# Attention weights made transposed by a second score product, in place of six transposes

## The chip, the cores and the metric

The kernel runs on one core of a Trainium2 chip. The metric is the device time of the whole program in microseconds (us), measured outside the profiler; three executions of the kernel before gave 4838.08, 4842.09 and 4854.21, so the median is 4842.09 us. A profile is one more execution with the hardware profiler on. Engines: PE is TensorE (matrix products; PEld is its loading of stationary operands), DVE is VectorE, ACT is ScalarE, POOL is GpSimd, SP is SyncE, which here only issues DMAs.

## The reference, cut to what matters

Two Swin transformer blocks run one after the other on 32 images of 192 channels and 32 by 32 pixels. Each block is window attention and an MLP:

```
xn  = layernorm(x); shift by 4 pixels; cut into 8 x 8 windows (64 tokens, 12 heads of 16)
q, k, v = split(xn @ w_qkv + b_qkv)
attn = q @ k.T * 16 ** -0.5            (block 0 only: + relative position bias + shift mask)
attn = softmax(attn)
x   = x + unwindow(attn @ v) @ w_proj + b_proj
h   = gelu(layernorm(x) @ w_fc1 + b_fc1)
x   = x + h @ w_fc2 + b_fc2
```

## The kernel before, in words

The work goes by tiles of two windows: 128 tokens in the partitions. There are 8 tiles for an image and a block, and 32 x 2 x 8 = 512 tiles. Tiles are visited in groups of four; groups of block 0 of one image alternate with groups of block 1 of the image before (`group_order`). Every fp32 value that enters a product is split into a 16-bit high part and a low part (`..._hi`, `..._lo`), and products are summed over three of the four combinations.

The program is a hand-written software pipeline. All engines run the same loop `slot(s)`, each with its own list of steps in a fixed order, and every step waits on semaphores (`ge(name, n)`: wait until step `name` has been done for tile n). No scheduler moves anything: on an engine, what stands later in the slot waits for what stands earlier. The steps for one tile are spread over slots:

- slot s - 1 and before: layer norm (DVE `statistics`, `mean_variance`, `centre`; POOL `scale`, which raises the variance to the power -0.5 (L1036), and `normalise`, L1042), POOL `norm1_lo` (L1091), a DMA transpose `norm1_turn` (SP, L356), `qk_product` (PE, L448), `qk_hi` (ACT, L663), `qk_lo` (DVE, L877), and the DMA transpose `qk_turn` of q and k (SP, L379).
- slot s: `v_product` (PE, L481), `scores` (PE, L497 the bias table in block 0 only, and L506: 24 products of 64 x 64), `row_max` (DVE, L893), `shift_scores` (PE, L515: minus the row maximum, added in PSUM), `exp` (ACT, L677, from PSUM `ps_s` to `p_tok` in SBUF).
- slot s + 1: `p_transpose` (PE, L526: six fp32 transposes into PSUM `ps_t`), `p_hi` (ACT, L683, `ps_t` to `pt`), `p_lo` (DVE, L898, `ps_t` minus high part), and at the slot's end `pv_product` (PE, L543).
- slots s + 2 and s + 3: `o_norm` (DVE), `o_hi`, `o_lo` (POOL, L1066, L1071), DMA transpose `o_turn` (SP, L371), `projection` (PE), residual, second layer norm, `norm2_lo` (POOL, L1076), `norm2_turn` (SP, L364).

The MLP runs once for a group of four tiles, so slots have a place 0 to 3 (`mlp_phase`). At place 0 PE makes `hidden(0)`, `(1)`, `(2)`, then `pv_product`, then `hidden(3)` (L569, five products of 512 columns each, in the two halves of `ps_s` in turn), and at the head of place 1 `hidden(4)` and `(5)`. ACT's `gelu(m)` (L691) empties each one; `hidden(m)` waits for `gelu(m - 2)`. POOL and DVE split the result (`hidden_hi`, L1098; `hidden_lo`, L931). ACT loads another function table before the first GELU of a group and before the next exponential (L702, L697). At places 1, 2 and 3 PE makes `mlp_out` (L581), and at place 2 twice, once ahead of `shift_scores`; its residual (DVE, L918) there stands ahead of `centre`.

Three orders matter below. ACT in a slot: ..., `v_hi`, `p_hi(s - 1)`, `exp(s)`, at place 0 the GELU table and `gelu(0)`, then `qk_hi(s + 2)`. DVE: ..., `row_max(s)`, `v_lo`, `mean_variance`, `centre(s + 3)`, `p_lo(s - 1)`, `qk_lo(s + 2)`. SP: `qk_turn(s + 1)`, `norm1_turn(s + 3)`, `norm2_turn(s - 3)`, `o_turn(s - 1)`, then a load or store of pixels; so `qk_turn` of one slot stands right behind the three other transposes of the slot before.

## Time and profile before

| | us |
|---|---|
| median of three runs | 4842.09 |
| the profiled execution | 4850.49 |
| its span | 4848.1 |
| PE busy | 4275.9 (88%) |
| DVE busy | 3373.7 (70%) |
| POOL busy | 2997.4 (62%) |
| ACT busy | 2773.6 (57%) |

The span is from the first to the last instruction of the program; 2.4 us lie around it. 512 slots in 4848.1 us are 9.5 us each on average, but slots differ: a slot at place 0 holds twenty products of 512 columns and is longer than the others. Of the span, 4700 us (from 100 to 4800) are the steady pipeline. Busy time is the union of an engine's instructions; a busy PE is not PE at its peak, since a product's recorded end lies behind the start of the next. TensorE's granted clock was 0.979 of 2.4 GHz on average: 2.4 GHz with short stretches of 1.2 GHz.

### The profile page before, as it was taken

How to read it: one execution, taken by the hardware profiler on the slowest of the kernel's cores; microseconds unless marked ns; L12 is line 12 of the kernel's file. 1: busy time of each engine (PE TensorE's matmuls, PEld its weight loads, DVE VectorE, ACT ScalarE, POOL GpSimd, SP SyncE). 2: the span in 40 equal slices, each digit the busy share in tenths (PEclk: the TensorE clock that was granted, in tenths of full speed). 3: DMA queues.
4: the chain of work that ended last, by engine and by line, in shares of the span. 5: the costliest groups of instructions: out<-in, count | busy, mean ns of one | idle time of the engine just before them, and what ended most of it. 6: DMA issues, size and time to landing. Idle time of an engine off the chain costs nothing.

```text
span 4848.1 us, 175812 instructions
## 1 busy us (share of the span) xinstructions
PE 4275.9 (88%) x66384; PEld 3016.7 (62%) x66384; DVE 3373.7 (70%) x9081; ACT 2773.6 (57%) x5921; POOL 2997.4 (62%) x6254
## 2 busy tenths in 40 slices
PE   4888888898899989898889898999888988898987
PEld 2566666666666666666666666666666666666665
DVE  5666676667677767776667776777776777677765
ACT  1555555556566556565556555656555555565654
POOL 4666666666666666666566666666665666666654
PEclk9999999999999999999999999999999999999999
DMA  4445444444444544444444454444454444444543
GB/s 95 84 84 88 82 88 89 87 82 88 89 89 88 93 86 89 92 87 86 86 88 87 87 91 88 87 91 89 87 88 85 87 87 89 87 86 88 88 81 58
DMA packets 1560580, 420.58 MB, mean 87 GB/s; under 512 B 1457462, under 2 KB 1558202, under 8 KB 1559740
## 3 DMA queue, kind: packets, MB, share of 16 engines
q1 hardware_dynamic: 1559740, 409.35, 46.3%
q8 instruction: 531, 8.70, 0.7%
q14 instruction: 309, 2.53, 0.2%
HBM read 31.56 MB, written 25.17 MB: 12 GB/s over the span
## 4 chain that ended last, share of the span: by engine, by line
PE 45%; DMA 13%; POOL 10%; issue 10%; DVE 9%; SPq 9%; ACT 2%; DVEq 0%; POOLq 0%; ACTq 0%
PE ps_s L569 12%; DMA qkt<-qk 9%; PE bank L581 8%; PE bank L448 6%; PE bank L543 4%; POOL hid L1098 4%; DVE smax L893 3%; SPq L356 3%; SPq L371 3%; PE ps_t L526 2%; PE ps_s L515 2%; DVE hid L931 2%; POOL xs L1091 2%; DMA ht<-xs 2%; PE ps_s L506 2%
## 5 line engine op out<-in xcount | busy, mean ns | idle before, releaser
L1036 POOL TENSOR_TENSOR rstd<-vare,half 128x2 f32<-128x2 f32 x518 | 359.1, 693 | 1138.1 <-DVE vare L871 1138.1
L931 DVE TENSOR_TENSOR hid<-hid 128x512 f16<-128x512 f32 x768 | 600.6, 782 | 511.5 <-POOL hid L1098 491.4
L569 PE MATMUL ps_s<-ht,w_fc 128*128 128x512 f16 x3840 | 879.8, 382 | 18.6 <-DMA ht<-xs 10.1
L581 PE MATMUL bank<-w_fc,hid 128*128 128x192 f16 x9216 | 851.8, 247 | 7.5 <-DVE hid L931 5.5
L581 PEld LDWEIGHTS bank<-w_fc,hid 128*128 128x128 f16 x9216 | 774.6, 98 | 80.5 <-issue 53.2
L893 DVE TENSOR_REDUCE smax<-ps_s 128x12 bf16<-128x768 f32 x512 | 488.2, 954 | 453.3 <-PE ps_s L506 442.8
L683 ACT ACTIVATE pt<-ps_t 128x768 f16<-128x768 f32 x512 | 414.8, 810 | 598.7 <-PE ps_t L526 595.6
L1098 POOL TENSOR_SCALAR hid<-hid 128x512 f16<-128x512 f32 x768 | 561.8, 732 | 297.0 <-ACT hid L691 295.9
L691 ACT ACTIVATE hid<-ps_s,b_fc 128x512 f32<-128x512 f32 x768 | 529.6, 690 | 333.8 <-PE ps_s L569 158.6
L569 PEld LDWEIGHTS ps_s<-ht,w_fc 128*128 128x128 f16 x3840 | 361.1, 98 | 464.0 <-issue 69.5
L448 PE MATMUL bank<-w_qkv,xt 128*128 128x384 f16 x2560 | 530.5, 340 | 25.0 <-DMA xt<-xs 23.2
L672 ACT ACTIVATE v_blk<-bank 64x192 f16<-64x192 f32 x1024 | 334.2, 326 | 292.0 <-PE bank L481 285.5
L898 DVE TENSOR_TENSOR pt<-ps_t,pt 128x768 f16<-128x768 f32 x512 | 489.5, 956 | 14.8 <-issue 1.3
L677 ACT ACTIVATE p_tok<-ps_s 128x768 f32<-128x768 f32 x512 | 417.4, 815 | 138.0 <-PE ps_s L515 137.6
L663 ACT ACTIVATE qk<-bank 128x384 f16<-128x384 f32 x1024 | 448.3, 495 | 72.5 <-PE bank L450 70.1
L526 PE MATMUL ps_t<-ident,p_tok 128*128 128x128 f32 x3072 | 467.1, 290 | 0.1
L656 ACT ACTIVATE xs<-xn 128x192 f16<-128x192 f32 x512 | 184.8, 361 | 478.1 <-POOL xn L1042 477.3
L877 DVE SCALAR_TENSOR_TENSOR qk<-bank,qk 128x192 f16<-128x192 f32 x1024 | 316.5, 351 | 183.7 <-ACT qk L663 183.7
L543 PEld LDWEIGHTS bank<-v_blk,pt 128*64 128x64 f16 x18432 | 333.3, 113 | 119.5 <-issue 119.5
L448 PEld LDWEIGHTS bank<-w_qkv,xt 128*128 128x128 f16 x2560 | 255.9, 101 | 226.7 <-issue 73.8
L515 PE MATMUL ps_s<-smax,neg_ident 128*128 128x384 bf16 x1024 | 270.2, 348 | 141.3 <-DVE smax L893 137.7
L543 PE MATMUL bank<-v_blk,pt 128*64 128x34 f16 x18432 | 383.9, 185 | 3.7 <-DVE pt L898 3.4
(113 smaller groups left out, 7420.9 us busy)
## 6 DMA issues: line engine op xcount, KB each, us to landing
x_img<-in_x_dram SPq DMA_DIRECT2D x256, 96.0 KB, 2.2
out_dram<-y_img SPq DMA_DIRECT2D x256, 96.0 KB, 1.9
xt<-xs SPq DMA_TRANSPOSE x512
qkt<-qk SPq DMA_TRANSPOSE x512, 3.9
ot<-os SPq DMA_TRANSPOSE x512, 2.4
ht<-xs SPq DMA_TRANSPOSE x512, 2.3
stage<-in_L_conv_fc_w_dram SPq DMA_DIRECT2D x2, 384.0 KB, 4.2
stage<-in_L_conv_w_fc_dram SPq DMA_DIRECT2D x2, 384.0 KB, 3.9
```

The lines of the kernel that those rows point to most:

```text
L448: last = mm(dst, blocks[:, blk, :], w[:, part, n0:n1], start=(i == 0), stop=(i == 4 and bias is None))
L526: last = nc.tensor.transpose(ps_t[:, g // 3, (g % 3) * TOK:(g % 3 + 1) * TOK], p_tok[:, n % 2, g].rearrange("p a k -> p (a k)"), ident[:, :])
L543: last = mm(ps_o[rows, g * 2 * VW:(g + 1) * 2 * VW].rearrange("p (a d) -> p a d", a=2), pt[:, n % 2, ps, g, rows], v_blk[:, n % 2, vs, :, ...
L569: last = mm(ps_s[:, u % 2, :], w_fc1[layer][:, part, m * 128:(m + 1) * 128], ht[:, p % 2, blk, :], start=(i == 0), stop=(i == 4))
L581: mm(bank[:, 0:C], hid16[:, hs, m, tok], w_fc2[layer][:, ws, m, :], start=(m == 0 and i == 0), stop=False)
L663: last = copy(qk[:, n % 2, i * HEADS:(i + 1) * HEADS, places, :], src.broadcast_to([128, HEADS, 2, HD]), ACT.Copy, scale=UNSCALE)
L677: nc.scalar.activation(p_tok[:, n % 2].rearrange("p g a k -> p a g k"), ps_s[:, :, 0:PAIRS * WIN].rearrange("p a (g k) -> p a g k", g=PAIR ...
L691: nc.scalar.activation(hid[:, u % 2, :], ps_s[:, u % 2, :], ACT.Gelu, bias=b_fc1[layer][:, m:m + 1], scale=UNSCALE).then_inc(S["gelu"], 1)
L893: v.tensor_reduce(smax[:, n % 2], ps_s[:, :, 0:PAIRS * WIN].rearrange("p a (g k) -> p a g k", g=PAIRS), AX.X, ALU.max).then_inc(S["max_don ...
L898: v.tensor_tensor(pt[:, n % 2, 1].rearrange("p (b g) t -> p b (g t)", b=2), ps_t[:, :, 0:3 * TOK], pt[:, n % 2, 0].rearrange("p (b g) t -> ...
L931: v.tensor_tensor(hid16[:, 1, m, :], hid[:, u % 2, :], hid16[:, 0, m, :], ALU.subtract)\
L1098: g_.tensor_scalar(hid16[:, 0, m, :], hid[:, u % 2, :], 1.0, 0.0, ALU.mult, ALU.add)\
```

## The change

The scores are made twice. The first time as before, tokens of the query in the partitions, only to take the row maximum. The second time (`scores_turned`) with the operands exchanged, so that the keys are in the partitions of `ps_t`; the bias, in block 0, is added by 12 products of 128 columns, and the row maximum is subtracted there by 12 products of 128 columns instead of two of 384. The exponential then reads `ps_t` and writes P already transposed, as fp32, to `p_exp` in SBUF. The six transposes go. `p_hi` moves behind `exp` of the same tile, and `p_hi` and `p_lo` read `p_exp` in SBUF, where they read `ps_t` in PSUM. `ps_s` is released by `row_max` instead of `exp`.

```
-        p_tok = sb("p_tok", [128, 2, PAIRS, 2, WIN], F32)
+        p_exp = sb("p_exp", [128, 2, PAIRS * TOK], F32)
...
 def scores(n):
-                    ge("exp_done", n - 1)
+                    ge("max_done", n - 1)
...
+                def scores_turned(n):
+
+                    _, layer, t = visit(n)
+                    ge("exp_done", n - 1)
+                    if layer == 0:
+                        for g in range(PAIRS):
+                            for par in range(2):
+                                mm(ps_t[par * 64:par * 64 + 64, g // 3, g % 3 * TOK:(g % 3 + 1) * TOK],
+                                   bias_tab[:, par, g, :], pair_ident[:, :],
+                                   start=(g % 3 == 0), stop=False, skip_group_check=True)
+                    else:
+                        pe.nop(nofuse=True)
+                    for g in range(PAIRS):
+                        for w in range(2):
+                            for par in range(2):
+                                rows = slice(par * 64, par * 64 + 64)
+                                tok = slice(w * WIN, (w + 1) * WIN)
+                                place = g % 3 * TOK + w * WIN
+                                last = mm(ps_t[rows, g // 3, place:place + WIN],
+                                          qkt[rows, n % 2, PAIRS + g, tok], qkt[rows, n % 2, g, tok],
+                                          start=(layer == 1 and g % 3 == 0 and w == 0), stop=False, skip_group_check=True)
+                    last.then_inc(S["t_mm"], 1)
+
                 def shift_scores(n):
 
                     ge("max_done", n)
-                    for par in range(2):
-                        last = mm(ps_s[:, par, 0:PAIRS * WIN].rearrange("p (g k) -> p g k", g=PAIRS), neg_ident[:, :],
-                                  smax[:, n % 2, par, :].unsqueeze(2).broadcast_to([128, PAIRS, WIN]),
-                                  start=False, stop=True, skip_group_check=True)
+                    for g in range(PAIRS):
+                        for par in range(2):
+                            last = mm(ps_t[par * 64:par * 64 + 64, g // 3, g % 3 * TOK:(g % 3 + 1) * TOK],
+                                      smax[:, n % 2, par, g:g + 1].broadcast_to([128, WIN]), neg_ident[:, :],
+                                      start=False, stop=True, skip_group_check=True)
                     last.then_inc(S["shift"], 1)
-
-                def p_transpose(n):
...
 def hidden(m):
-                        ge("exp_done", min(s, ENDS))
+                        ge("max_done", min(s, ENDS))
...
 PE, slot(s):
-                if live(s - 1):
-                    p_transpose(s - 1)
+                if live(s):
+                    scores_turned(s)
...
                 def exp(n):
+                    ge("p_lo", n - 2)
                     ge("shift", n)
-                    nc.scalar.activation(p_tok[:, n % 2].rearrange("p g a k -> p a g k"),
-                                         ps_s[:, :, 0:PAIRS * WIN].rearrange("p a (g k) -> p a g k", g=PAIRS),
+                    nc.scalar.activation(p_exp[:, n % 2].rearrange("p (a t) -> p a t", a=2), ps_t[:, :, 0:3 * TOK],
                                          ACT.Exp).then_inc(S["exp_done"], 1)
 
                 def p_hi(n):
-                    ge("tp", n)
-                    copy(pt[:, n % 2, 0].rearrange("p (b g) t -> p b (g t)", b=2), ps_t[:, :, 0:3 * TOK], ACT.Copy)\
+                    ge("exp_done", n)
+                    copy(pt[:, n % 2, 0].rearrange("p g t -> p (g t)"), p_exp[:, n % 2], ACT.Copy)\
                         .then_inc(S["p_hi"], 1)
...
 ACT, slot(s):
-                if live(s - 1):
-                    p_hi(s - 1)
...
                 if live(s):
                     exp(s)
+                    p_hi(s)
...
                 def p_lo(n):
                     ge("p_hi", n)
-                    v.tensor_tensor(pt[:, n % 2, 1].rearrange("p (b g) t -> p b (g t)", b=2), ps_t[:, :, 0:3 * TOK],
-                                    pt[:, n % 2, 0].rearrange("p (b g) t -> p b (g t)", b=2), ALU.subtract)\
+                    v.tensor_tensor(pt[:, n % 2, 1].rearrange("p g t -> p (g t)"), p_exp[:, n % 2],
+                                    pt[:, n % 2, 0].rearrange("p g t -> p (g t)"), ALU.subtract)\
                         .then_inc(S["p_lo"], 1)
```

What this does to the order of instructions is shown at two places. The first is ACT in a slot at place 0, before: `xs` is `norm2_hi`, `v_blk` is `v_hi`, `pt<-ps_t` is `p_hi` of the tile before, `p_tok<-ps_s` is `exp`, `spare` goes with the table load, `hid` is `gelu`, `qk` is `qk_hi`.

```order
L656 ACTIVATE xs<-xn 128x192
L672 ACTIVATE v_blk<-bank 64x12x16 x2
L683 ACTIVATE pt<-ps_t 128x768
L677 ACTIVATE p_tok<-ps_s 128x2x6x64
L702 ACT_TABLE_LOAD
L702 ACTIVATE spare<-half 1x1
L691 ACTIVATE hid<-ps_s,b_fc 128x512
L663 ACTIVATE qk<-bank 128x12x32
L663 ACTIVATE qk<-bank 128x24x16
L691 ACTIVATE hid<-ps_s,b_fc 128x512 x3
```

The same place on ACT, changed; `p_exp<-ps_t` is `exp` and `pt<-p_exp` is `p_hi`, now of the same tile.

```order
L670 ACTIVATE xs<-xn 128x192
L686 ACTIVATE v_blk<-bank 64x12x16 x2
L692 ACTIVATE p_exp<-ps_t 128x768
L697 ACTIVATE pt<-p_exp 128x768
L716 ACT_TABLE_LOAD
L716 ACTIVATE spare<-half 1x1
L705 ACTIVATE hid<-ps_s,b_fc 128x512
L677 ACTIVATE qk<-bank 128x12x32
L677 ACTIVATE qk<-bank 128x24x16
L705 ACTIVATE hid<-ps_s,b_fc 128x512 x3
```

The number of instructions is the same; `p_hi` went from ahead of the exponential to between it and the table load, `gelu(0)` and `qk_hi`.

The second place is PE in a slot at place 2 of block 0, before: `bank<-w_qkv,xt` with 96 columns is `v_product`, then the bias, the scores, the transposes of the tile before, `mlp_out`, `shift_scores`, `qk_product`.

```order
L481 MATMUL bank<-w_qkv,xt 64x96 x20
L497 MATMUL ps_s<-bias_tab,pair_ident 128x384 x2
L506 MATMUL ps_s<-qkt 64x64 x24
L526 MATMUL ps_t<-ident,p_tok 128x128 x6
L581 MATMUL bank<-w_fc,hid 128x192 x18
L583 MATMUL bank<-b_out,bias_rows 128x192
L515 MATMUL ps_s<-smax,neg_ident 128x384 x2
L448 MATMUL bank<-w_qkv,xt 128x384 x5
```

The same place on PE, changed.

```order
L481 MATMUL bank<-w_qkv,xt 64x96 x20
L497 MATMUL ps_s<-bias_tab,pair_ident 128x384 x2
L506 MATMUL ps_s<-qkt 64x64 x24
L518 MATMUL ps_t<-pair_ident,bias_tab 64x128 x12
L529 MATMUL ps_t<-qkt 64x64 x24
L595 MATMUL bank<-w_fc,hid 128x192 x18
L597 MATMUL bank<-b_out,bias_rows 128x192
L539 MATMUL ps_t<-neg_ident,smax 64x128 x12
L448 MATMUL bank<-w_qkv,xt 128x384 x5
```

Six transposes are replaced by 36 products in block 0 (24 in block 1, without L518), and the two shift products by twelve. On DVE, POOL and SP the order of the steps is unchanged.

## Rows read from the trace of the kernel before

**Rows 1.** Waits of the whole span: engine line <- releaser: us, times, longest.

```profile
ACT pt L683 <- PE ps_t L526: 595.6, 385, 5.1
...
PE ps_s L497 <- DMA qkt<-qk: 161.2, 158, 3.0
...
PE ps_s L515 <- DVE smax L893: 137.7, 293, 1.1
...
PE ps_s L506 <- issue: 131.3, 123, 3.2
```

**Rows 2.** Chain that ended last, 2440 to 2464: start, length, what.

```profile
2440.96 1.20 PE ps_s L569 x5
...
2449.76 0.71 POOL rstd L1036
...
2453.11 1.18 SPq L356
...
2454.45 1.63 SPq L364
...
2458.23 5.26 DMA qkt<-qk
...
2463.63 0.80 PE ps_s L497 x2
```

**Rows 3.** Timeline, two slots at place 0: start, length, instruction, idle before.

```profile
2399.05 0.81 ACT L677 ACTIVATE p_tok<-ps_s 128x768 f32<-128x768 f32 x1
...
2400.00 3.40 PE L569 MATMUL ps_s<-ht,w_fc 128*128 128x512 f16 x15 [0.16 <-ACT p_tok L677]
...
2401.28 0.69 ACT L691 ACTIVATE hid<-ps_s,b_fc 128x512 f32<-128x512 f32 x1
...
2435.60 0.81 ACT L677 ACTIVATE p_tok<-ps_s 128x768 f32<-128x768 f32 x1
...
2436.89 3.40 PE L569 MATMUL ps_s<-ht,w_fc 128*128 128x512 f16 x15 [0.35 <-DMA ht<-xs]
...
2438.16 0.69 ACT L691 ACTIVATE hid<-ps_s,b_fc 128x512 f32<-128x512 f32 x1 [0.24 <-PE ps_s L569]
```

**Rows 4.** Timeline of PE, 2450.7 to 2454.8.

```profile
2452.03 0.25 PE L450 MATMUL bank<-b_out,bias_rows 128*128 128x192 f16 x1
2452.21 0.62 PE L481 MATMUL bank<-w_qkv,xt 128*64 128x96 f16 x20
...
2453.62 0.38 PE L506 MATMUL ps_s<-qkt 64*64 64x64 f16 x24
2453.94 0.88 PE L526 MATMUL ps_t<-ident,p_tok 128*128 128x128 f32 x6
2454.65 0.33 PE L581 MATMUL bank<-w_fc,hid 128*128 128x192 f16 x2
```

**Rows 5.** Costliest groups of the page: count, busy us, mean ns, idle us and what ended it.

```profile
L569 PE MATMUL ps_s<-ht,w_fc 128*128 128x512 f16 x3840 | 879.8, 382 | 18.6 <-DMA ht<-xs 10.1
...
L893 DVE TENSOR_REDUCE smax<-ps_s 128x12 bf16<-128x768 f32 x512 | 488.2, 954 | 453.3 <-PE ps_s L506 442.8
```

**Rows 6.** Timelines of DVE and POOL where the two run together.

```profile
2445.28 0.96 DVE L931 TENSOR_TENSOR hid<-hid 128x512 f16<-128x512 f32 x1 [0.58 <-POOL hid L1098]
...
2445.66 0.79 POOL L1066 TENSOR_SCALAR os<-o_tok 128x192 f16<-128x192 f32 x1
...
2449.65 0.96 DVE L898 TENSOR_TENSOR pt<-ps_t,pt 128x768 f16<-128x768 f32 x1
...
2456.84 0.95 DVE L898 TENSOR_TENSOR pt<-ps_t,pt 128x768 f16<-128x768 f32 x1
...
2457.08 0.69 POOL L1036 TENSOR_TENSOR rstd<-vare,half 128x2 f32<-128x2 f32 x1 [2.10 <-DVE vare L871]
```

**Rows 7.** Single lines: count, duration ns min/median/max.

```profile
L1036 POOL TENSOR_TENSOR rstd<-vare,half x518: 688/692/699, 77.2 to 4815.7; 128x2 f32<-128x2 f32 x173
...
L1066 POOL TENSOR_SCALAR os<-o_tok x512: 347/352/892, 102.8 to 4809.5; 128x192 f16<-128x192 f32 x171
```

More of the change, by code:

```diff
@@ L225, in swin_program @@
             "centred rstd bn1a bn1 ln1 hi1 lo1 qk_mm v_mm mask_set qk_hi qk_lo v_hi v_lo "
-            "s_mm max_done shift exp_done tp p_hi p_lo pv inv_done o_norm o_hi o_lo "
+            "s_mm t_mm max_done shift exp_done p_hi p_lo pv inv_done o_norm o_hi o_lo "
             "pr resid1 bn2a bn2 ln2 hi2 lo2 fc2 resid2".split(), TOTAL)
@@ L511, in shift_scores @@
                 def shift_scores(n):
                     ge("max_done", n)
-                    for par in range(2):
-                        last = mm(ps_s[:, par, 0:PAIRS * WIN].rearrange("p (g k) -> p g k", g=PAIRS), neg_ident[:, :],
-                                  smax[:, n % 2, par, :].unsqueeze(2).broadcast_to([128, PAIRS, WIN]),
-                                  start=False, stop=True, skip_group_check=True)
-                    last.then_inc(S["shift"], 1)
-                def p_transpose(n):
-                    ge("p_lo", n - 1)
-                    ge("exp_done", n)
-                    for g in range(PAIRS):
-                        last = nc.tensor.transpose(ps_t[:, g // 3, (g % 3) * TOK:(g % 3 + 1) * TOK],
-                                                   p_tok[:, n % 2, g].rearrange("p a k -> p (a k)"), ident[:, :])
-                    last.then_inc(S["tp"], 1)
+                    for g in range(PAIRS):
[3 more added lines that the diff above has]
+                                      start=False, stop=True, skip_group_check=True)
```

2 lines of the change are left out of this document (1 added, 1 removed).

## The prediction, made before the changed kernel had run

> **What bounds the kernel now.** I read the table of busy times first: PE is busy 88% of the span, but no engine is full, so the waits and the chain must say what a removed PE instruction is worth.
>
> The waits come next [rows 1]. PE waits for three things. Two are one: the scores wait for q and k, turned by DMA (161.2 us in block 0; in block 1 the wait stands as 131.3 us of "issue", since a no-op takes it). The third is the row maximum ahead of the shift, 137.7 us in 293 of 512 slots. And ACT waits 595.6 us for the transposes ahead of `p_hi`: `p_hi` stands in time in which ACT has nothing else.
>
> Then the chain [rows 2]. It is one loop over a group of four slots: PE makes the hidden layer (place 0, head of place 1); `centre` follows the row maximum; POOL raises to a power (L1036), normalises, splits (L1091); SP issues three transposes and then the one of q and k; 5.26 us later that has landed and PE's scores start. From L1036 to the scores (POOL, then SP's transposes one behind the other, of which the chain's rows show two) everything is in order and nothing waits for PE. The same holds one slot later, from place 2, where `mlp_out` ahead of the shift also stands in the chain, since its residual precedes `centre`. So a group's time is: hidden layer, then twice this row through DVE, POOL, SP and DMA. A delay in it counts 1:1; PE work beside it counts nothing.
>
> **Part 1: the transposes go, the second scores come (PE).** Six transposes take 0.71 us (from 2453.94 to 2454.65 [rows 4]). The scores there take 0.32 for 24, on four quarters of the array at once. The turned ones use only the two quarters on the diagonal, so a pair costs its 64 columns at 2.4 GHz, 0.027 and a little: 0.36 for 12 pairs; 0.32 to 0.64 are the bounds (as packed as before; each by itself). In block 0 come 12 bias products of 128 columns on half the array. Products of 96 columns there (L481) take about (0.62 - 0.21)/19 = 0.022 each [rows 4], 0.21 being the length of one, so 0.043 for a pair, which is 96 columns at 2.4 GHz: pairs overlap. For 128 columns that makes 0.057 a pair, 0.34 for the six (0.64 if they don't overlap). Entering the half array costs something: L450 to L481 is 0.18 where a product of 192 columns takes 0.08, so 0.10 a change of shape; block 0 gets two more (0.20). The one change from the scores to full-size products is there before and after, and between 24 and 24 products of one shape there is none. Block 1: 0.36 - 0.71 = -0.35. Block 0: 0.36 + 0.34 + 0.20 - 0.71 = +0.19, with a first pair that does not overlap (0.06) +0.25.
>
> The Trainium skill (TensorEngine Tiling (Array Packing), Key Properties) says that a change of tiling mode drains the engine. The 0.10 us of the row agrees with that.
>
> Where does this count? At places 0, 1 and 3 the shift waits for the row maximum: 0.95 for the reduction [rows 5] and some 0.1 for the semaphores, 1.05 against the 0.71 that PE now fills. In block 1 the second scores make this wait longer, not the slot shorter; in block 0 0.96 just fit. At place 2 `mlp_out` covers the maximum, so the difference counts: +0.25 in 64 groups, -0.35 in 64, -6 us together, less than the terms are sure to: I take 0.
>
> **Part 2: the shift.** Twelve products of 128 columns in pairs, 0.34 plus two changes of shape, against two of 384 columns, 0.32: +0.2 (0 to +0.4) on PE in each slot. It delays `qk_product` and what follows; ahead of the scores at places 0, 2 and 3 PE waits anyway, mean (161.2 + 131.3)/512 = 0.57, and at place 0 ACT comes to set the pace (part 3). I take 0.
>
> **Part 3: `p_hi` between `exp` and `gelu(0)` (ACT).** Nothing hides it there. At place 0, `hidden(2)` needs the half of `ps_s` that `gelu(0)` empties. Five products of 512 columns take 1.08 (5 x 512 at 2.4 GHz, and a little), so `hidden(2)` starts 2.16 after `hidden(0)`: 2402.16 and 2439.05 [rows 3]. `gelu(0)` ends at 2401.97 and 2438.85: just ahead, and L569 shows 18.6 us of idle time in 3840 products, 10.1 of it for a DMA [rows 5]. `p_hi` is 0.81 now, perhaps 0.85 from SBUF. In the first slot `gelu(0)` then ends 0.82 later, 2402.79, with 0.07 for the semaphore 2402.86: `hidden(2)` 0.70 late. In the second, `gelu(0)` had itself waited 0.24 for PE, so it moves by 0.6: 0.45 late. I take 0.60 (bounds 0.45 and 0.82). Behind it are `pv_product`, `hidden(3)` and the splits of `gelu(0)` on POOL and DVE, all later by the same; PE runs without a gap there, so nothing takes it back. 128 groups x 0.60 = +77 us. That `hidden(0)` may start at the row maximum instead of the exponential gives at most the 0.16 of the first slot, and ACT decides anyway. At other places ACT has idle time, `qk_hi` comes some 0.6 later, and `qk_turn` has its order on SP, not `qk_lo`, ahead of it.
>
> **Part 4: `p_lo` reads two operands from SBUF (DVE against POOL).** Its length stays near 0.96. But today, with one operand in PSUM, it runs beside POOL's L1036 (2456.84 and 2457.08 [rows 6]), and L1036 is 688 to 699 ns in all 518 cases [rows 7]: no contention. The one DVE instruction with two SBUF operands is L931. POOL's L1066 starts inside it at 2445.66, takes 0.79 where its median is 0.352, and ends at 2446.45, 0.21 behind the DVE's end at 2446.24 [rows 6, 7]: POOL stood until the DVE was done, and then ran. So POOL gets a lock. `p_lo` starts right behind `centre`, and L1036 0.24 later at place 2 (0.11 at place 1), each time. If L1036 must wait likewise, it ends at 2457.79 + 0.21 + (0.692 - 0.352) = 2458.34 instead of 2457.77: +0.57. This lies in the chain [rows 2]. From place 1 it reaches the scores of place 3 (there 2450.61 + 0.55 = 2451.16 instead of 2450.46, +0.70 [rows 2, 6]), from place 2 those of place 0. The scores of place 0 come after both, so of 0.57 and 0.70 one counts, and PE has slack between place 3 and place 0: I take 0.57 a group, 128 x 0.57 = +73 us. The lower bound is 0 (L1036 reads two numbers, perhaps late), the upper 0.70.
>
> The Trainium skill (SBUF — State Buffer, SBUF: two separate sides) has this as a rule: a DVE operation with two SBUF inputs and a GpSimd operation that reads SBUF take a shared port pair as an exclusive lock, and the later one blocks for the whole instruction. By that rule the term is the +73, without it 0. The L1066 row agrees; no row here shows it for L1036.
>
> **The sum.** 77 + 73 + 0 = +150 us on 4850.5 of the profiled execution; this stands 8.4 above the median of the runs, so 4842 + 150 = 4992.
>
> **The rivals.**
> - No lock on L1036: only part 3. 4842 + 77 = 4919. For it: two elements; against: the lock holds whoever reads.
> - Packing fails, products of the half array go one by one: at place 2 +0.57 more in block 0 (0.30 bias, 0.28 scores) and +0.27 in block 1, and +0.3 in each shift, which at place 0 delays `exp` and `gelu(0)`: (0.87 + 0.57) x 64 = 92 more, 5085. L481's 0.043 a pair speaks against it. Longer waits could also grant 1.2 GHz more often: the product at 2463.63, behind a long wait, took 0.80 for two of 384 columns [rows 2].
> - Faster: PE's own work sets the end everywhere, and both delays are absorbed. The shift and the changes of shape hide, and it is -0.71 + 0.36 in 512 slots and +0.34 in 256: -92, so 4750. It decides if `gelu(0)` had over 0.8 us of slack. PE's 88% speaks for it; against it, 137.7 us of waits for the maximum [rows 1] and slack of 0.19 and 0.20 ahead of `hidden(2)` [rows 3].
> - No change within measurement: the delays fall into SP's slack and place 2 cancels. 4842.
>
> **How the numbers follow.** Forecast 0.58, no lock 0.16, packing or clock 0.14, faster 0.08, no change 0.04. The range takes the forecast's bounds and both slower rivals: low end 128 x 0.45 = 58 less what may be gained at place 2, 4890; high end 5085. A change under 0.3%, 15 us, can't be told from none. Faster 0.08, same 0.04, slower 0.88.
>
> **What would show it.** Right: PE's L583 (`hidden`) gets some 75 us of waits for ACT's `gelu` where now there are next to none; POOL's power goes from 692 to about 1260 ns; `p_lo` stays at 0.96; the wait of the shift for the row maximum grows in block 1; the scores still wait for q and k. Wrong: a power that stays at 692 strikes part 4; a `hidden` without waits strikes part 3; bias or shift products at over 0.04 us each strike parts 1 and 2.

## The result and the profile after

The changed kernel takes 5151.3 us (median of four runs, 5148.27 to 5166.43), the kernel before 4845.2 (four runs, 4838.08 to 4854.21): ratio 1.0637, 95% interval 1.0609 to 1.0665. The forecast was 4992 with a range up to 5085. The direction was right; the cost is 309 us where 150 were forecast. (Here and below a cost in us is the ratio less 1, times 4845.)

The page of the changed kernel: span, busy times and instruction counts, and the DMA queue that loads code.

```profile
span 5146.1 us, 210883 instructions
...
PE 4383.1 (85%) x83792; PEld 3113.3 (60%) x83792; DVE 3298.2 (64%) x9081; ACT 2790.2 (54%) x5921; POOL 3284.7 (64%) x6254
...
q8 instruction: 666, 10.91, 0.9%
```

The same of the kernel before.

```profile
PE 4275.9 (88%) x66384; PEld 3016.7 (62%) x66384; DVE 3373.7 (70%) x9081; ACT 2773.6 (57%) x5921; POOL 2997.4 (62%) x6254
...
q8 instruction: 531, 8.70, 0.7%
```

PE has 107 us more to do and the span grew by 298, so most of the loss is waiting. Two things to see: POOL is busy 287 us longer with the same 6254 instructions, and the program is longer, so 135 more pieces of code are loaded.

The costliest groups of the page (columns as in rows 5).

```profile
L1049 POOL TENSOR_TENSOR rstd<-vare,half 128x2 f32<-128x2 f32 x518 | 644.8, 1245 | 1111.2 <-DVE vare L884 1111.2
...
L583 PE MATMUL ps_s<-ht,w_fc 128*128 128x512 f16 x3840 | 909.8, 388 | 55.6 <-issue 27.6
...
L906 DVE TENSOR_REDUCE smax<-ps_s 128x12 bf16<-128x768 f32 x512 | 488.2, 953 | 477.6 <-PE ps_s L506 472.8
...
L890 DVE SCALAR_TENSOR_TENSOR qk<-bank,qk 128x192 f16<-128x192 f32 x1024 | 318.7, 353 | 441.7 <-ACT qk L677 437.4
L911 DVE TENSOR_TENSOR pt<-p_exp,pt 128x768 f16<-128x768 f32 x512 | 487.4, 952 | 1.5 <-issue 1.5
...
L697 ACT ACTIVATE pt<-p_exp 128x768 f16<-128x768 f32 x512 | 431.8, 843 | 16.2
```

POOL's power (L1049) takes 1245 ns on average where it took 692 [rows 7]; `p_lo` (L911) stays at 952, and `p_hi` (L697) takes the 0.84 that was reckoned with. The rest of POOL hardly changed: 518 x 0.553 = 286 of its 287 us are this one line.

Waits of the whole span, PE, after [rows 1].

```profile
PE ps_s L497 <- DMA qkt<-qk: 195.1, 157, 3.1
PE ps_s L506 <- issue: 163.7, 140, 3.1
PE ps_t L539 <- DVE smax L906: 160.4, 248, 1.5
PE bank L448 <- DMA xt<-xs: 73.0, 74, 4.6
```

These four waits have all grown. The last row is `qk_product` waiting for the turned normalised rows, which was 23 us before.

PE at place 1, block 0 [rows 4]: start, length, instruction.

```profile
2438.39 0.38 PE L506 MATMUL ps_s<-qkt 64*64 64x64 f16 x24
2438.70 0.53 PE L518 MATMUL ps_t<-pair_ident,bias_tab 128*64 128x128 f16 x12
2439.16 0.56 PE L529 MATMUL ps_t<-qkt 64*64 64x64 f16 x24
2439.66 0.42 PE L604 MATMUL bank<-ident,x_tok 128*96 128x128 f32 x2
```

From L518's start to L604's the second scores take 0.96 us. The forecast was 0.34 + 0.36 + 0.20 for two changes of shape + 0.06 = 0.96. The products pack as reckoned.

DVE and POOL, one slot [rows 6].

```profile
2454.53 0.95 DVE L911 TENSOR_TENSOR pt<-p_exp,pt 128x768 f16<-128x768 f32 x1
...
2454.77 1.26 POOL L1049 TENSOR_TENSOR rstd<-vare,half 128x2 f32<-128x2 f32 x1 [5.77 <-DVE vare L884]
```

POOL starts 0.24 after `p_lo` and ends 0.55 behind `p_lo`'s end; alone it takes 0.69. It stood for 0.57, as L1066 did in rows 6.

The chain that ended last, from the power of place 2 to q and k [rows 2]: start, length, what.

```profile
2454.77 1.27 POOL rstd L1049
...
2457.70 0.53 POOL xs L1104
...
2458.35 1.18 SPq L356
...
2459.68 1.18 SPq L364
...
2461.00 1.62 SPq L371
...
2462.72 0.52 SPq L298
...
2463.44 3.81 DMA qkt<-qk
```

It is the chain of rows 2, with a longer first row. And L371, the issue of a transpose by SP, takes 1.62 where its two neighbours take 1.18 (more of that below).

Idle time ahead of `hidden` (PE and its weight loads, added up): releaser, us, times; before, and then after.

```profile
  ACT hid L691: 49.6, 256
```

```profile
  ACT hid L705: 121.8, 299
```

That is +72 us, and it looks like the 75 that the prediction expected. But this view adds the waits of the products and those of the weight loads, which lie side by side, and 49.6 were there already, all of them of weight loads. The products alone wait (before: no such row):

```profile
PE ps_s L583 <- ACT hid L705: 26.4, 47, 1.0
```

What a delay did is read better from start to start. From the first product of `hidden(0)` to the first of `hidden(2)` it takes 2.19 us before and 2.65 now (means of 96 slots): 0.46 later, where 0.60 was taken. From the last product of `hidden(3)` to the scores of place 1 it takes 4.05 in both kernels, so what is lost up to there is lost by the slot. And `hidden(0)` itself starts 3.87 behind the scores instead of 3.29. These 0.58 no term of the prediction has; `qk_product`, just ahead of it, starts 0.86 behind the shift where it was 0.47 (see the code loading below).

**Slots.** The table gives, from the traces, the mean time from the first scores product of a slot to that of the next (tiles 63 to 446, 96 slots for each place), TensorE's granted clock, and the sum of its stretches at 1.2 GHz.

| kernel | cost, us | place 0 | 1 | 2 | 3 | clock | us at 1.2 GHz |
|---|---|---|---|---|---|---|---|
| before | 0 | 12.25 | 7.87 | 9.01 | 7.72 | 0.979 | 203 |
| l1_lock_place1 | 63 | 12.14 | 7.99 | 9.68 | 7.69 | 0.972 | 274 |
| l2_lock_place2 | 71 | 12.38 | 7.91 | 8.93 | 8.38 | 0.975 | 250 |
| l3_lock_place3 | 11 | 12.47 | 7.93 | 9.01 | 7.73 | 0.981 | 192 |
| e2_lock_only | 109 | 12.51 | 7.95 | 9.41 | 8.02 | 0.973 | 270 |
| e3_act_only | 42 | 12.65 | 7.87 | 8.94 | 7.73 | 0.982 | 178 |
| h1_lock_act_shift | 162 | 12.86 | 8.02 | 9.30 | 7.89 | 0.980 | 202 |
| n1_no_lock | 299 | 13.21 | 8.71 | 9.08 | 8.30 | 0.963 | 386 |
| n3_three_out | 214 | 12.74 | 8.49 | 9.14 | 8.25 | 0.953 | 479 |
| n5_three_out_filler | 158 | 12.51 | 8.55 | 9.08 | 7.96 | 0.986 | 144 |
| g1_best | 194 | 12.65 | 8.22 | 9.66 | 7.80 | 0.974 | 267 |
| after | 309 | 13.30 | 8.27 | 9.47 | 8.18 | 0.964 | 370 |

Every place of the changed kernel is 0.40 to 1.05 us longer. Costs are medians of several executions and slots are those of the profiled one; the profiled executions of l1 and l2 are the slowest of their four (4918.96 and 4932.45), so their slots show more than their cost.

### The profile page after: what moved, and what is told of

Same layout as the page of the kernel before. It is cut to its first block, busy times and chain, and to the rows that moved or that the text cites. A ratio compares the mean times of both kernels' runs of the same rounds, so it can differ in the third digit from the quotient of the medians.

```text
span 5146.1 us, 210883 instructions
## 1 busy us (share of the span) xinstructions
PE 4383.1 (85%) x83792; PEld 3113.3 (60%) x83792; DVE 3298.2 (64%) x9081; ACT 2790.2 (54%) x5921; POOL 3284.7 (64%) x6254
## 4 chain that ended last, share of the span: by engine, by line
PE 41%; DMA 13%; issue 12%; POOL 11%; SPq 9%; DVE 9%; ACT 4%; POOLq 0%; DVEq 0%; ACTq 0%
PE ps_s L583 10%; DMA qkt<-qk 9%; PE bank L595 8%; PE bank L448 7%; DMA xt<-xs 4%; DVE smax L906 4%; PE bank L557 4%; POOL hid L1111 3%; SPq L371 3%; POOL rstd L1049 3%; PE ps_t L539 3%; ACT hid L705 2%; DVE hid L944 2%; SPq L364 2%; POOL xs L1104 2%
## 5 line engine op out<-in xcount | busy, mean ns | idle before, releaser
L1049 POOL TENSOR_TENSOR rstd<-vare,half 128x2 f32<-128x2 f32 x518 | 644.8, 1245 | 1111.2 <-DVE vare L884 1111.2
L692 ACT ACTIVATE p_exp<-ps_t 128x768 f32<-128x768 f32 x512 | 415.0, 811 | 1013.5 <-PE ps_t L539 1011.4
L583 PE MATMUL ps_s<-ht,w_fc 128*128 128x512 f16 x3840 | 909.8, 388 | 55.6 <-issue 27.6
L595 PE MATMUL bank<-w_fc,hid 128*128 128x192 f16 x9216 | 870.7, 250 | 7.3 <-DVE hid L944 6.1
L448 PE MATMUL bank<-w_qkv,xt 128*128 128x384 f16 x2560 | 555.3, 352 | 74.6 <-DMA xt<-xs 73.0
L911 DVE TENSOR_TENSOR pt<-p_exp,pt 128x768 f16<-128x768 f32 x512 | 487.4, 952 | 1.5 <-issue 1.5
L697 ACT ACTIVATE pt<-p_exp 128x768 f16<-128x768 f32 x512 | 431.8, 843 | 16.2
L539 PE MATMUL ps_t<-neg_ident,smax 128*64 128x128 bf16 x6144 | 287.0, 233 | 173.6 <-DVE smax L906 160.4
L448 PEld LDWEIGHTS bank<-w_qkv,xt 128*128 128x128 f16 x2560 | 221.0, 102 | 250.3 <-issue 121.0
L900 DVE SCALAR_TENSOR_TENSOR v_blk<-bank,v_blk 64x192 f16<-64x192 f32 x1024 | 361.6, 353 | 6.8
```

The lines of the kernel that those rows point to most:

```text
L448: last = mm(dst, blocks[:, blk, :], w[:, part, n0:n1], start=(i == 0), stop=(i == 4 and bias is None))
L539: last = mm(ps_t[par * 64:par * 64 + 64, g // 3, g % 3 * TOK:(g % 3 + 1) * TOK], smax[:, n % 2, par, g:g + 1].broadcast_to([128, WIN]), ne ...
L583: last = mm(ps_s[:, u % 2, :], w_fc1[layer][:, part, m * 128:(m + 1) * 128], ht[:, p % 2, blk, :], start=(i == 0), stop=(i == 4))
L595: mm(bank[:, 0:C], hid16[:, hs, m, tok], w_fc2[layer][:, ws, m, :], start=(m == 0 and i == 0), stop=False)
L911: v.tensor_tensor(pt[:, n % 2, 1].rearrange("p g t -> p (g t)"), p_exp[:, n % 2], pt[:, n % 2, 0].rearrange("p g t -> p (g t)"), ALU.subtr ...
L1049: g_.tensor_tensor(rstd[:, m % 2, :], vare[:, m % 2, :], half[:, :].broadcast_to([128, 2]), ALU.pow)\
```

## The experiments

**One cost at a time.** Theory A is the sum on record; theory B says that delays count at more places than it has.

e1_phi_back: the changed kernel with `p_hi` at its old place.

```
+                if live(s - 1):
+                    p_hi(s - 1)
                 exp(s) ...
-                    p_hi(s)
```

> The changed kernel with one step moved: p_hi(s - 1) on ACT again where the kernel before had it, ahead of exp(s); the rest as changed. Theory A (p_hi ahead of gelu(0) costs 0.60 to 0.85 us in each of 128 groups, and it stands in one chain with everything else): 77 to 110 us less than the changed kernel's 5151, so 5040 to 5075, and hidden no longer waits for gelu (121.8 us of waits go to near 0). Theory B (the other terms already cover it, since the groups are bound by POOL, SP and DMA): 5130 to 5150, the wait turns up at the scores.

Measured 5099.8 us, ratio 1.0509 (1.0465 to 1.0552): 62 less than the changed kernel (the two intervals leave 28 to 97). Between the two theories. Most of the loss is elsewhere.

e2_lock_only: the kernel before, with both operands of `p_lo` in SBUF.

```
-v.tensor_tensor(pt[..., 1], ps_t[:, :, 0:3 * TOK], pt[..., 0], ALU.subtract)
+v.tensor_tensor(pt[..., 1], p_tok[:, n % 2], pt[..., 0], ALU.subtract)
```

> The kernel before, with p_lo on DVE reading p_tok in SBUF in place of ps_t in PSUM (so the low part that it makes is not that of P transposed), and exp waiting for p_lo of two tiles before, which is long done; nothing else. Theory A (the delay of POOL's power by the lock, 0.57, counts once a group, as predicted): +73 us, 4915. Theory B (it counts in series at places 1, 2 and 3, since each has a transfer of its own behind POOL: q and k for place 3, q and k for place 0, x for the q and k product of place 0): two to three times that, 4985 to 5060. POOL's power goes to 1.26 us in both.

Measured 4964.0, ratio 1.0225 (1.0184 to 1.0267): 109 us (89 to 129). The low part is not that of P transposed here. The lock is real, without any other part of the change, and costs half as much again as the 73 on record.

e3_act_only and e23_both: the kernel before, with an additional copy of 768 elements on ACT behind `exp` at place 0; and that together with the lock.

```
+copy(pad_out[:, p % 2], pad_in[:, :], ACT.Copy)   # place 0, between exp and gelu(0)
```

> The kernel before, with one more ACT copy of 768 fp32 elements to fp16, from a buffer of its own to another, behind exp at place 0 only, ahead of the GELU table. Theory A: 0.60 us a group, +77 us, 4920. Theory B (the hidden layer had slack): under +20 us.

> The kernel before with both: p_lo from SBUF and the ACT copy behind exp at place 0 (its low part is again not that of P transposed). If the two delays stand in one chain, the sum of both runs' gains; if they run beside each other, the larger alone. Theory B of the lock: within 40 us of the changed kernel's 5151, what is left being PE's work and the clock. Theory A of the lock: 4990, and PE's added work costs the other 150.

Measured 4886.2, ratio 1.0086 (1.0055 to 1.0118), 42 us (27 to 57) where 77 were forecast; together 4985.3, ratio 1.0277 (1.0243 to 1.0312), 134 us. `hidden` waits for ACT as in the changed kernel. The trace of e3, first in the view that adds products and weight loads, then the products alone:

```profile
  ACT hid L693: 140.3, 338
```

```profile
PE ps_s L571 <- ACT hid L693: 30.8, 82, 0.4
```

The first is 91 us more than before, but it counts twice. From `hidden(0)` to `hidden(2)` it takes 2.54 us instead of 2.19 (means), 0.35 x 128 = 45 us, and that is the cost: the delay counts in full, but it is smaller than the 0.60 forecast. In the median slot it is 0.55. In a fifth of the slots there is none: there the exponential ends 0.87 us ahead of `hidden(0)`, elsewhere 0.29, so `gelu(0)` has a lead when `hidden(0)` starts.

**Where does the lock count?** l1, l2 and l3 make e2's edit in the slots of one place alone.

```
+src = ps_t[:, :, 0:3 * TOK]
+if place == 1:                     # l2: 2, l3: 3
+    src = p_tok[:, n % 2] ...
```

> The kernel before, with p_lo reading p_tok (two operands in SBUF) in the slots of place 1 alone; there the low part is not that of the transposed P. In each of 128 groups POOL's power of place 1 should take about 1.26 us instead of 0.69 and reach, over the queries and keys, the scores of place 3. The step on record (of the delays of places 1 and 2 one counts, because PE has slack between places 3 and 0): 0 to +15 us here, 4842 to 4860. The rival (each lock is paid in the slot it lands on, because every slot behind it is itself set by a chain and not by PE): 0.57 less what of it is covered, so +0.3 to +0.5 us a group, 4885 to 4910.

> The same in the slots of place 2 alone, whose power is in the chain to the scores of place 0. The step on record: this is the one delay that counts, 0.57 x 128 = +73 us, 4915. The rival: it is one of three that add up to the 117 us of all of them, so +35 to +50 us, 4880 to 4895.

> The same in the slots of place 3 alone. The power of place 3 gives the normalised rows whose transposes qk_product of place 0 waits for; the step on record did not count it: within 10 us of before. The rival: hidden(0) and all that is behind it in the slot of place 0 start later, +25 to +40 us, 4870 to 4885. The three of these runs together should give the 117 us of the run in which p_lo reads p_tok in every slot; if their sum is far below 117, the delays reinforce one another, if it is far above, they cover one another.

Measured: 4909.6, ratio 1.0129 (1.0105 to 1.0153), 63 us; 4920.4, 1.0147 (1.0123 to 1.0170), 71 us; 4858.3, 1.0023 (1.0006 to 1.0040), 11 us. The power in l1 has the old time in most slots and the new one in those of place 1: count, duration ns min/median/max.

```profile
L1040 POOL TENSOR_TENSOR rstd<-vare,half x518: 688/693/1269, 77.8 to 4884.3; 128x2 f32<-128x2 f32 x173
```

The low part is not that of P transposed in the slots named. Place 2 alone gives 71, the 73 on record; place 3 nearly nothing, as on record. But place 1 costs almost as much as place 2, and not 0 to 15. The delay can be followed through SP. Means over the slots, us from the start of a slot's scores:

| | before | l1 | l2 | after |
|---|---|---|---|---|
| place 1: POOL's last `xn` ends | 6.36 | 6.94 | 6.36 | 6.93 |
| place 1: `norm1_turn` issued | 7.02 | 7.55 | 7.02 | 7.55 |
| place 2: `o_turn` issued | 1.94 | 2.48 | 1.93 | 2.33 |
| place 2: `qk_turn` issued | 4.19 | 4.71 | 4.22 | 4.56 |
| place 2: slot ends (scores of place 3) | 9.02 | 9.70 | 8.94 | 9.48 |
| place 3: `qk_turn` issued | 2.76 | 2.29 | 3.39 | 3.20 |
| place 3: slot ends (scores of place 0) | 7.71 | 7.70 | 8.36 | 8.17 |

In l1 POOL's delay of 0.58 is 0.53 at `norm1_turn`, 0.54 at `o_turn`, 0.52 at `qk_turn` and 0.68 at the scores of place 3; the slot behind it stays at 7.70. In l2 the same happens one slot later. The slack that the prediction counted on was there, and it was used: PE's idle time ahead of the scores of place 0 is 0.74 us before and 0.35 in l1 (means). But PE finished later too. Ahead of the scores of place 3 it now waits 1.46 us instead of 0.97, and in the slot behind this wait TensorE ran at 1.2 GHz for 1.72 us on average, where it was 0.59. The slots of place 3 that are free of 1.2 GHz take 7.29 us (50 slots; 7.46 in 73 slots before). So, by these rows, the delay made the wait longer, and the half clock behind the wait used the slack up; no run takes the clock out of l1. Singly the three sum to 145 and together (e2) to 109, so they cover each other in part, by 36; the step "of the two one counts" would have them cover each other by 63.

**The shift and the bias.** f1_shift12: the kernel before with the shift in twelve products; f2_no_second_bias: the changed kernel without the twelve bias products.

```
-last = mm(ps_s[:, par, 0:PAIRS * WIN], neg_ident, smax[:, n % 2, par, :] ...)   # x2
+for g in range(0, PAIRS, 2):                                                  # f1, x12
+    for w in range(2): mm(ps_s[rows, par, g * WIN:(g + 2) * WIN], neg_ident[:, rows], ...)
```

> The kernel before, with the shift made by twelve products of 128 columns on half the array in place of two of 384 (same result, still in ps_s); nothing else. Theory A (as predicted: +0.15 to 0.2 us on PE in each of 512 slots, of which waits for q and k take nearly all): under +20 us, 4865 at most. Theory B (the shift stands in the chain at places 0 and 1, and what PE does later pushes transfers that follow): 0.15 in two to four slots of a group, +38 to +77 us, 4885 to 4925.

> The changed kernel without the 12 bias products in scores_turned of block 0 (P of block 0 then lacks the relative bias, while the maximum has it). Theory A (they count at place 2 only, where the maximum is covered by mlp_out): 64 groups x 0.5, 32 us less than 5151, about 5120. Theory B (they count at every place of block 0): 256 x 0.5, some 130 us less, 5020.

Measured: f1 4880.8, ratio 1.0078 (1.0050 to 1.0105), 38 us where the record has 0. f2 5114.7, ratio 1.0555 (1.0522 to 1.0588), 40 us less than the changed kernel (the intervals leave 10 to 69), near the expected 32. The slots don't show it where the expectation had it: in f2's profile the slot of place 2 is not shorter (9.62 us, 9.47 in the changed kernel), and places 0, 1 and 3 are shorter by about 0.1 each. The twelve products take 0.47 us where two took 0.34; 0.13 x 512 = 67 us on PE, of which half counts.

**Do the costs add?** h1_lock_act_shift is e23 and f1 together.

> The kernel before with three things of the change and without the second scores: p_lo reads p_tok (the low part is not that of the transposed P), ACT makes an additional copy of 768 elements behind exp at place 0, and the shift is made of twelve products of 128 columns. Alone or together these gave +139 us (lock and ACT) and +36 us (shift). If the costs add, 5015 to 5030. If they lie beside one another, since each makes other waits longer that would hide the next, about 4990. If longer waits lower TensorE's clock and so add a cost of their own, over 5040.

Measured 5008.8, ratio 1.0334 (1.0308 to 1.0360): 162 us, against 134 + 38 = 172. They add. These are the three terms of the prediction, and its sum for them was 150. The other 147 us of the change lie outside them.

**The clock.** f3 and f4 put eight products with an identity ahead of the wait of the scores for q and k, at places 0, 2 and 3, in the kernel before and after; they write spare columns that nobody reads.

```
+if mlp and place in (0, 2, 3):
+    for _ in range(8):
+        mm(ps_s[:, 0, 3 * TOK:4 * TOK], ident16, ident16, start=True, stop=True)   # f3: ps_t
```

> The kernel before with eight products of 128 columns (the identity by itself, into columns of ps_t that nothing reads) ahead of PE's wait for q and k at places 0, 2 and 3, where it stands idle 0.6 to 1 us a slot. Theory A (stretches at 1.2 GHz follow from such waits and cost PE time that counts): the 203 us at 1.2 GHz fall to under 100 and the time falls by up to 50 us, 4795 to 4830. Theory B (the clock falls for other reasons, or what it costs lies in waits anyway): the time stays or grows by what the products add where there is no wait, 4840 to 4870.

> The changed kernel with the same eight products ahead of the same waits, into columns of ps_s that nothing reads. Theory A (of the 306 us, some 80 are the clock, as 370 us at 1.2 GHz stand against 203): the time at 1.2 GHz falls by half or more and the time to 5060 to 5110. Theory B: the time stays at 5150.

Measured: f3 4857.9, ratio 1.0019 (1.0000 to 1.0038), clock 0.993 for 0.979, and no gain. f4 5103.2, ratio 1.0536 (1.0495 to 1.0577), clock 0.982 for 0.964: 49 us less than the changed kernel. In the changed kernel TensorE is at 1.2 GHz for 370 us instead of 203, and that costs. That f3 gained nothing does not show that the half clock was free before: its slots of places 3 and 0 are 0.16 and 0.15 us shorter, and those of places 1 and 2 are 0.20 and 0.18 longer, perhaps since the eight products there stand in the way. A second reading agrees in size. Slots free of 1.2 GHz take 36.37 us for the four places before and 38.46 in the changed kernel, 2.09 x 128 = 267 us more; all slots together show 303. So about 36 us lie in the slots at half clock, and 267 do not.

**Costs taken away from the changed kernel.** n1_no_lock makes the low part from `p_exp` alone; n3_three_out is that with e1's and f2's edits; h3_phi_other puts `p_hi` back at places 1 to 3 only.

```
-v.tensor_tensor(pt[..., 1], p_exp[:, n % 2], pt[..., 0], ALU.subtract)
+v.tensor_scalar(pt[..., 1], p_exp[:, n % 2], 2.0 ** -12, None, ALU.mult)
```

> The changed kernel, with the low part made as p_exp times 2^-12 in place of p_exp less p_hi: one operand in SBUF instead of two, the output of the same size (the low part is not that of P). If it is the two SBUF operands that lock POOL out, POOL's power goes from 1.25 back to about 0.69 us, and the time falls by what the lock costs in this kernel: by the additive sum 110 to 117 us, 5035 to 5045; if the lock costs more where ACT and PE are late too, under 5020. If the power stays at 1.25 us, a DVE operation locks POOL for another reason than its second operand, and the time stays at 5150, less what a shorter p_lo gives (10 us).

> The changed kernel without the lock (as in the run before this), with p_hi(s - 1) at its old place on ACT, and without the twelve bias products of the second scores (P of the blocks with a bias is made without it). What is left of the change is the twelve products of the shift and the second scores in place of the transposes. If the costs add: 5151 - 113 - 51 - 37 = 4950. Then 100 us are left beside the kernel before, of which the shift is 36 and 65 would be a cost that no term of the working has. If the delays reinforce one another (each of them also lengthens the waits of the others, and the stretches at 1.2 GHz), what is left is little: the shift less what block 1 gains at place 2, 4850 to 4890.

> The changed kernel, with p_hi at its old place on ACT in the slots that follow, except behind exp of place 0. If p_hi behind exp costs at place 0 above all (the 39 us of the run with the additional copy there), moving the other three gives 12 us: 5140. If the other places cost as much or more (ACT's qk_hi comes later, and DVE waits 437 us for it in the changed kernel against 184 us before), it gives 30 to 50 us: 5100 to 5120, and the place 0 part would be small here.

Measured: n1 5144.2, ratio 1.0618 (1.0591 to 1.0644), 10 us less than the changed kernel and not distinguishable from it. n3 5062.1, ratio 1.0441 (1.0407 to 1.0475), 95 less, where the three alone give 10 + 62 + 40 = 112: taken away, too, the costs about add. h3 5134.7, ratio 1.0604 (1.0577 to 1.0630), 16 less, close to the 12 of the reading that place 0 is the main one, but not distinguishable from the changed kernel either (the intervals leave -10 to +43). n1 failed as a test of the lock, and the trace says why: single lines of POOL and DVE, and one slot.

```profile
L1049 POOL TENSOR_TENSOR rstd<-vare,half x518: 689/863/875, 77.7 to 5117.2; 128x2 f32<-128x2 f32 x173
```

```profile
L911 DVE TENSOR_SCALAR pt<-p_exp x512: 550/553/570, 99.4 to 5106.5; 128x768 f16<-128x768 f32 x171
```

```profile
2445.29 0.55 DVE L911 TENSOR_SCALAR pt<-p_exp 128x768 f16<-128x768 f32 x1
...
2445.53 0.86 POOL L1049 TENSOR_TENSOR rstd<-vare,half 128x2 f32<-128x2 f32 x1 [4.59 <-DVE vare L884]
```

With one source in SBUF the DVE's operation runs at twice the rate (553 ns for 952) and still holds POOL: the power ends 0.55 behind the DVE's end, as with two sources. The lock got shorter, not absent. The Trainium skill (SBUF — State Buffer, SBUF: two separate sides) names this case too: a DVE operation in a two-port performance mode takes the shared pair as well. The trace agrees.

Yet the power is 0.39 shorter and nothing came of it. Place 2 gained 0.39 and place 1 lost 0.44. At place 1 `qk_turn` is issued at 3.85, as in the changed kernel (3.86), but the scores start 4.86 later instead of 4.41: the transfer had landed after 4.50 us on average instead of 4.05. Why it was slower is open. From place 2 the scores start 5.36 later instead of 4.90, but there the transfer is no slower (4.38, and 4.35 in the changed kernel); PE itself is not ready (it stands 0.52 us ahead of these scores instead of 0.93).

**What is left.** g1_best is the changed kernel in a better order, with all its computation; n5 and g2 are n3 and g1 with f4's eight products.

```
 place 0: p_hi(s) not behind exp(s) but ahead of exp(s + 1)
 places 2, 3, 0: p_lo(s - 1) ahead of row_max(s), no longer beside the power
```

> The changed kernel arranged anew, with its whole computation: p_hi stays behind exp at places 1, 2 and 3 but waits for the next slot at place 0, and p_lo goes ahead of the row maximum at places 2, 3 and 0, so that it no longer lies on POOL's power. If the lock and ACT's delay at place 0 are two separate costs and p_lo costs nothing ahead of the maximum: 5151 - 110 - 39 = 5000. If p_lo delays the maximum, which the shift waits for, by up to 0.95 us in some of the slots: 5060 or more. Below the kernel before (4849) it comes by neither.

> The kernel of n3_three_out (5062) with eight identity products of 128 columns ahead of the wait for q and k at places 0, 2 and 3, in spare columns of ps_s. n3_three_out still stands 220 us above the kernel before, and its trace has 479 us of TensorE at 1.2 GHz against 203. Theory clock: where the same products brought the changed kernel 48 us (370 to 185 us at 1.2 GHz), here there is more to have, 80 to 140 us: 4920 to 4980, with the granted clock up from 0.953 to about 0.98. Theory no clock: the half clock lies in stretches that nothing waits for, and the products only fill a wait: 5040 to 5070, as they gave nothing in the kernel before (203 to 66 us at 1.2 GHz, ratio 1.0019).

> The arrangement of g1_best (5040, 267 us at 1.2 GHz, whole computation) with the same eight products. Theory clock: 0 to 40 us less, 5000 to 5040, since g1_best has little more of the low clock than the kernel before. It stays above the kernel before in either case; if it came within 50 us of it, the costs named so far would be nearly all order and clock, and not work.

Measured: g1 5039.8, ratio 1.0401 (1.0350 to 1.0452), 115 less than the changed kernel; n5 4996.8, ratio 1.0327 (1.0285 to 1.0369), 56 less than n3, with the clock at 0.986 for 0.953; g2 5007.3, ratio 1.0358 (1.0327 to 1.0389), the best version of the whole computation, and still 173 us above the kernel before. Groups of g1's page:

```profile
L914 DVE TENSOR_TENSOR pt<-p_exp,pt 128x768 f16<-128x768 f32 x512 | 526.7, 1029 | 0.0
...
L1054 POOL TENSOR_TENSOR rstd<-vare,half 128x2 f32<-128x2 f32 x518 | 432.8, 835 | 950.3 <-DVE vare L887 950.3
```

The power's mean falls from 1245 to 835 (one place of four is still locked, 692 + 0.25 x 570 = 835), and `p_lo` now meets other work of POOL at times (1029 for 952). n3 to n5 gives the clock 56 of the 214, less than the 80 to 140 expected; 158 stay, where single costs explain 38 (shift) and part of the lock.

**Code loading.** This is argued from rows and not from a run of its own. The change adds 17,408 products to PE, 34,816 instructions with their weight loads, and the queue that loads code moves 135 more pieces of 16 KB (531 to 666): one for 258 instructions. f1 adds 5120 products, and 572 pieces are loaded. A piece moves beside the pixels and the transposes. An `o_turn` issue (L371) takes 1.18 us in most slots, but over 1.3 us in:

| | before | f1 | after |
|---|---|---|---|
| pieces of code | 531 | 572 | 666 |
| long issues of `o_turn`, of 512 | 84 | 130 | 174 |
| of these, a piece started in them or up to 1.5 us ahead | 80 | 128 | 170 |
| short issues with such a piece | 33 of 428 | 25 of 382 | 39 of 338 |
| long less short, us | 0.71 | 0.70 | 0.75 |

A long issue almost always has a piece of code beside it, a short one seldom. The row of 1.62 in the chain above is one. But a long issue does not cost its 0.7 us. A straight-line fit of the length of a group of four slots to its number of long issues of the three transposes (96 groups, each compared with groups at the same point of the image) gives for one more long `o_turn` 0.26 us (standard error 0.11) before, 0.30 (0.14) in f1 and 0.16 (0.19) in the changed kernel, and for one more long `norm2_turn` 0.55 (0.20) in the changed kernel. So its 90 more of the first and 27 more of the second are worth some 14 + 15 us, and the 46 more of f1 some 14 of its 38. The count also moves by itself: e2 loads as much code as the kernel before (532 pieces) and has 65 long ones for 84, and g1 has 202 and is 115 us faster than the changed kernel. f3 has 3032 more products and 24 more pieces and costs 9 us (0 to 18), its clock being better.

A piece that starts while a transpose is moving costs more. At place 0 `qk_product` needs the rows that `norm1_turn` turned at the end of place 3. In the changed kernel this issue came less than 1.6 us ahead of the scores, and a piece started 0.8 to 2.3 us behind it, in 19 of 96 slots: there `qk_product` starts 2.11 us behind the shift, against 0.49 in the 20 slots with an issue as late and no such piece. `hidden(0)` stands right behind it. That is 19 x 1.62 / 96 x 128 = 41 us for the program. Before there are 2 such slots (1 us), in h1 13 with a smaller loss (1.38 against 0.62, 13 us). This is most of the 73.0 us of the row `PE bank L448 <- DMA xt<-xs` above, and a part of the 0.58 by which `hidden(0)` is late.

For q and k the evidence is mixed. From issue to the scores of place 2 it takes n1 5.26 us in 63 slots in which a piece started from 1.5 us ahead of the issue to 4 us behind it, and 4.09 in 33 without. But by the same measure the kernel before has a piece in 82 slots and takes 4.36 there, so the mere presence of a piece does not explain n1. A kernel with the same work and a longer program would settle what code loading costs; none was run.

## Why the prediction was wrong

**The step that failed: the terms that were taken at nothing.** The prediction adds up 77 for ACT, 73 for the lock and 0 for the shift, 150 us. h1 has these three, as far as the kernel before can have them, without the rest of the change, and costs 162 (149 to 174). The measured change costs 309, so nearly the whole miss, 147 of 159 us, lies in what the sum has at 0 or not at all: the second scores in place of the transposes (part 1, "I take 0"), `p_hi` at places 1 to 3 ("at other places ACT has idle time"), the clock, which stood only as a sentence in a rival, and the length of the program. What the runs show in their place: the twelve bias products 40 us (f2; 10 to 69), the clock 49 (f4; 16 to 82), `p_hi` at the other places some 16 (h3, not clear of noise). The rest is open in part.

**Part 1 was right for PE's own time and wrong in what it left out.** The second scores take 0.96 us in block 0, pairs overlap, a change of shape costs 0.10. From the scores to PE's next other work at place 2 the medians moved by +0.24 and -0.31 (+0.25 and -0.35 on record), and at places 0, 1 and 3 the shift starts as early as before (the mean of each place within 0.03 us). But the shift of place 2 starts 0.49 us later in block 0 (2.63 to 3.12, means) and no earlier in block 1 (2.84 to 2.85). The gain of block 1, 0.35 x 64 = 22 us on record, didn't arrive at the shift.

**That the three terms came to 150 against 162 was luck.** Each was off, and the errors cancel:

- The lock, part 4: 109 for 73. Its mechanism was right, 1260 ns, and so was its size for place 2 alone, 71 us. Wrong was "of 0.57 and 0.70 one counts, and PE has slack between place 3 and place 0": place 1 alone costs 63 and place 2 alone 71. The slack was real (0.74 us of idle time, of which 0.39 was used), but the longer wait ahead of the scores of place 3 came with 1.72 us at 1.2 GHz in the slot behind it instead of 0.59. The cost of this step is 36 us.
- The shift, part 2, "PE waits anyway, I take 0": 38 (24 to 51), or 28 on top of the other two (h1 less e23). The twelve products are 0.13 us longer. That a wait was read as cover, as in part 4, fits this; f1 also loads 41 more pieces of code, and no run separates the two.
- ACT at place 0, part 3: 42 for 77, by e3. The term was mis-sized: `hidden(2)` is late by 0.35 us in the mean (0.46 in the changed kernel) and not by 0.60, since in some slots ACT has a lead; and what it is late counts in full. Moving `p_hi` as a whole costs 62 (e1; 28 to 97), which agrees with 42 and 16.

**Sizes that held.** `p_lo` at 0.95, `p_hi` at 0.84, POOL's power at 1260 ns. The sign "some 75 us of waits for ACT's `gelu`" seems to hold with +72 only in the view that adds weight loads; the products wait 26.4 us.

Sum with what the runs showed: lock and ACT at place 0 134, shift 28, bias 40, `p_hi` elsewhere 16, clock 49: 267 of 309. The 42 left are of the size of what the rows give to code loading outside h1 (41 - 13 = 28 us at `qk_product`, and the long issues), but no run separates them, and several terms have an interval of 30 us to either side. The terms overlap too: clock and code are also in the runs of the others.

## What to carry to other kernels

A term that is set to 0 because "it hides" needs a price and a bound like any other; here the terms at 0 made nearly the whole miss. When several engines pass a tile on in a loop, an engine's idle time is poor cover for a delay in that loop; ask of each wait whether its releaser is itself in the loop, and what a longer wait does to the clock behind it. Measure a delay from start to start and not by a view of idle time that adds products and weight loads. An operation moved to SBUF operands can stop another engine: look for every instruction that starts inside it, in every slot. Products added to PE are also instructions to load: count them, look which transfers have a piece of code beside them, and compare the slots with and without before giving each a price.

## What the runs showed of the hardware

- A DVE subtraction with two SBUF operands holds off a POOL power of two elements a partition: 692 to 1260 ns, ending 0.55 us behind the DVE. A DVE scaling of one fp32 SBUF source into fp16 (553 ns) does the same.
- The issue of a DMA transpose on SP takes 1.18 us, and some 0.7 longer where code is being loaded: 170 of 174 long `o_turn` issues have a piece beside them, and 39 of 338 short ones, in the changed kernel. By the fit above the program got longer by 0.16 to 0.30 us for each, not by 0.7.
- A piece of code that starts 0.8 to 2.3 us behind the issue of a transpose holds up what waits for it: `qk_product` of place 0 starts 2.11 us behind the shift in 19 such slots, 0.49 in 20 others as late.
- Pairs of products on half or quarter arrays run beside each other: twelve of 128 columns on half the array take 0.47 us to the start of what follows, and 24 of 64 x 64 on the two quarters of the diagonal start two every 0.032 us in the changed kernel's trace, where the first scores start four in that time on all four quarters.
- TensorE's stretches at 1.2 GHz begin in the slots of places 3 and 0 (46 of 52 before, 77 of 95 after), during or behind waits ahead of the scores; PE's longest idle stretch just ahead of them is 2.2 and 2.0 us in the median. Eight products of 128 columns there raised the clock from 0.979 to 0.993 without gain (ratio 1.0019), and from 0.964 to 0.982 with a gain of 49 us.
